# Fewer, larger groups of TensorE transposes in a gated cross-attention and mixture kernel

## The reference, cut to what matters

```
x = x + tanh(g_xattn) * cross_attention(layernorm(x), ctx)     # x: 4 x 512 x 1024
z = layernorm(x)
base  = z @ W_base.T + b_base                                  # 1024 x 1024
gate  = softmax(z @ W_gate.T)                                  # 8 experts
thr   = sigmoid(z @ W_thr + b_thr) * 0.125
w     = relu(gate - thr), normalised to sum 1
h     = z @ A_w.T                                              # 8 experts x rank 16 = 128
moe   = 2 * sum over experts of w * (h @ B_w.T)
out   = x + tanh(g_ffn) * (base + moe)
```

## Time and profile before

| | |
|---|---|
| three runs | 472.96, 473.60, 475.18 us; median 473.6 |
| profiled execution, first to last instruction | 473.6 us |
| TensorE busy | 468.0 us (99%) |
| DVE busy | 361.7 us (76%) |
| ACT busy | 173.8 us (37%) |
| POOL busy | 119.8 us (25%) |
| granted TensorE clock, mean | 1.000 |

### The profile page before, as it was taken

How to read it: one execution, slowest core, us unless ns; L and a number is a source line. 1 busy time by engine, 2 the same in 40 slices (tenths; PEclk the granted TensorE clock), 3 DMA queues, 4 the chain that set the end, 5 groups by cost and what they waited for, 6 DMA issues and landing times.

```text
span 473.6 us, 6945 instructions
## 1 busy us (share of the span) xinstructions
PE 468.0 (99%) x2481; PEld 399.3 (84%) x2481; DVE 361.7 (76%) x750; ACT 173.8 (37%) x349; POOL 119.8 (25%) x107
## 2 busy tenths in 40 slices
PE   8999999999999999999999999999999999999997
PEld 7898999998887888888888888878888888888886
DVE  1687996588888978879987888968777678877733
ACT  5847532332224305226334625342241421414300
POOL 0020511002344253345242406031230502205000
PEclk9999999999999999999999999999999999999999
DMA  8993129958576378576379640221405032050202
GB/s 320 412 408 118 76 90 389 405 183 286 197 246 248 133 252 283 193 292 229 141 273 419 277 144 36 81 98 46 133 1 175 4 89 90 2 177 1 89 1 89
DMA packets 22114, 84.40 MB, mean 178 GB/s; under 512 B 2624, under 2 KB 3904, under 8 KB 19264
## 3 DMA queue, kind: packets, MB, share of 16 engines
q1 hardware_dynamic: 21792, 83.81, 48.2%
q10 hardware_dynamic: 288, 0.15, 0.1%
HBM read 61.93 MB, written 22.02 MB: 177 GB/s over the span
## 4 chain that ended last, share of the span: by engine, by line
PE 78%; DVE 8%; DMA 8%; issue 3%; ACT 1%; POOL 1%; SPq 0%; DVEq 0%; ACTq 0%
PE bank L769 10%; PE bank L773 10%; PE bank L771 10%; PE bank L649 6%; PE bank L685 5%; PE bank L687 5%; PE bank L686 5%; PE bank L530 4%; PE bank L742 4%; DMA xst<-x_dram 3%; DMA T_low<-t_low_T 2%; DMA xz<-xt_dram 2%; DMA out_dram<-xs 2%; PE bank L599 2%; DVE wl_B L1438 1%
## 5 line engine op out<-in xcount | busy, mean ns | idle before, releaser
L1554 POOL TENSOR_TENSOR small<-small,tiny 128x1 f32<-128x1 f32 (+2 forms) x25 | 23.6, 942 | 167.1 <-DVE small L1183 137.9
L1534 DVE SCALAR_TENSOR_TENSOR xs<-bank,tiny,xs 128x512 f32<-128x512 f32 (+1 forms) x61 | 43.3, 739 | 20.6 <-PE bank L773 14.9
L685 PE MATMUL bank<-xth,gram 128*128 128x512 f32 x144 | 57.3, 398 | 0.0
L687 PE MATMUL bank<-xtl,gram 128*128 128x512 f32 x144 | 56.3, 391 | 0.0
L686 PE MATMUL bank<-xth,gram 128*128 128x512 f32 x144 | 56.1, 390 | 0.0
L769 PE MATMUL bank<-wh_B,zh 128*128 128x512 f32 x116 | 47.0, 405 | 0.1
L769 PE MATMUL bank<-wh_T,zh 128*128 128x512 f32 (+1 forms) x116 | 46.6, 402 | 0.0
L1582 POOL TENSOR_TENSOR sq_sum<-sq_sum,sq 128x512 f32<-128x512 f32 x24 | 32.0, 1333 | 56.5 <-DVE sq L1362 56.5
L773 PE MATMUL bank<-wh_B,zl 128*128 128x512 f32 x116 | 45.6, 393 | 0.0
L771 PE MATMUL bank<-wl_B,zh 128*128 128x512 f32 x116 | 45.4, 391 | 0.0
L773 PE MATMUL bank<-wh_T,zl 128*128 128x512 f32 (+1 forms) x116 | 44.7, 386 | 0.0
(11 more groups left out here) (200 smaller groups left out, 1133.2 us busy)
## 6 DMA issues: line engine op xcount, KB each, us to landing
xst<-x_dram SPq DMA_DIRECT2D x16, 512.0 KB, 4.4
xz<-xt_dram SPq DMA_DIRECT2D x16, 512.0 KB, 7.6
out_dram<-xs SPq DMA_DIRECT2D x14, 512.0 KB, 2.7
xa<-x_dram SPq DMA_DIRECT2D x12, 512.0 KB, 3.4
x<-xa SPq DMA_DIRECT2D x12, 512.0 KB, 3.0
xs<-x SPq DMA_DIRECT2D x12, 512.0 KB, 4.0
wq_raw<-wq_dram SPq DMA_DIRECT2D x8, 512.0 KB, 13.8
t_raw_T<-wb_dram SPq DMA_DIRECT2D x4, 1024.0 KB, 16.7
```

The lines of the kernel that those rows point to most:

```text
L685: pe.matmul(acc[:, :], gram[:, g, 0, :], xth[b % 2][:, r, :], start=r == ROWS[j][0], stop=False)
L687: done = pe.matmul(acc[:, :], gram[:, g, 0, :], xtl[b % 2][:, r, :], start=False, stop=r == ROWS[j][-1])
L1534: dve.scalar_tensor_tensor(out=xs[slot][:, cols], in0=bank[n_bank][:, 0:hi - lo], scalar=tg[:, 1:2], in1=xs[slot][:, cols], op0=ALU.mult, ...
```

## The change

It alters the list `stages` and the order in which the low parts of a pair are numbered.

1. `mt` of the two tiles: in pairs 2, 3, 4 and 7 they stood behind P2 and behind P6, one transpose each; both now stand behind P6. Pairs 1, 5 and 6 had both in one place already.
2. `zt` of a11 and a12, for the next pair, in pairs 1 to 6: they stood behind P7 and behind P3, four transposes each; both now stand behind P3, eight in a row.
3. With them move, on ACT and DVE, the high and low parts and all sums. DVE's order behind P7 and P3 was: low a11, s3, s2, low s1, low s3, low a12, s4, low s2, low s4. It is now: low a11, s3, s2, low a12, s4, low s1, low s3, low s2, low s4. Pair 0, which prepares pair 1, keeps the old order.

```diff
-        LOWS = ("a22", "a11", "s1", "s3", "a12", "s2", "s4")
+        LOWS = [("a22", "a11", "s1", "s3", "a12", "s2", "s4")] * (PLAIN + 1)
+        LOWS += [("a22", "a11", "a12", "s1", "s3", "s2", "s4")] * (NP - PLAIN - 1)
...
-            for name in (() if plain(p) else LOWS):
+            for name in (() if plain(p) else LOWS[p]):
...
                              3: [("zt", q, "a21"), ("zt", q, "a22"), ("xn", t1), ("sum_high", q, "s1"), ("bias", t0)],
-                             4: [("zt", q, "a11"), ("sum_high", q, "s3"), ("sum_high", q, "s2"), ("sum_low", q, "s1"),
-                                 ("sum_low", q, "s3")],
-                             5: [("zt", q, "a12"), ("sum_low", q, "s2"), ("sum_high", q, "s4"), ("bias", t1)],
+                             5: [("zt", q, "a11"), ("zt", q, "a12"), ("sum_high", q, "s3"), ("sum_high", q, "s2"),
+                                 ("sum_low", q, "s1"), ("sum_high", q, "s4"), ("bias", t1), ("sum_low", q, "s3"),
+                                 ("sum_low", q, "s2")],
                              6: [("sum_low", q, "s4")]}
...
-                extra = {2: [("mt", t), ("mt", t + 1)]} if attends else {1: [("mt", t)], 2: [("mt", t + 1)]}
+                extra = {2: [("mt", t), ("mt", t + 1)]}
```

## The result

| | before | changed |
|---|---|---|
| median of 6 runs | 473.97 us | 477.84 us |
| lowest to highest | 472.96 to 475.18 | 475.20 to 479.78 |

The ratio is 1.008, with a 95% interval of 1.006 to 1.0101: 3.9 us slower, where 4.4 was forecast (478.0 us). The changed kernel's six runs spread over 4.6 us, the six of before over 2.2; in the larger sets measured beside the experiments the kernel before spreads over 4.6 to 5.4 us.

The account below looks back on a forecast made before the run. TensorE was taken as the bound, with the store and load loop nearly as tight. Late loads cost 4.5 us in pairs 2 to 6, less 0.1 saved: +4.4 on 473.6 gives 478.0 us, range 474.5 to 481.0.

Parts of the forecast that it names:

- What bounds the kernel: TensorE, busy 99% with one wait of 0.2 us; nearly as tight, the loop from `fin` through stores and load to transposes.
- The saving on TensorE: Ten groups of transposes fewer on TensorE were to save 0.1 us, with bounds of -0.2 to 0.3.
- `fin` 2.2 us late, and not in pair 1: On DVE nine steps behind the eight transposes delay `fin` by 2.2 us; in pair 1 it is 0.2 us earlier.
- The delay passes to the landing, and from there to the transposes: The 2.2 us passes through stores and load to the second tile's landing in pairs 3 to 6, then stalls TensorE.
- The terms: TensorE's stalls in pairs 2 to 6: 0.2, 0.7, 0.8, 2.1 and 0.7 us, adding up to 4.5 us.
- The merging of `mt` makes it worse: The first four transposes now wait for the second tile too, not only the second four, which had 0.43 us more.
- The base: The time the loss is added to: the profiled span of 473.6 us, equal to the median of the runs.
- The delay isn't lost on the way: Rival: the delay gets lost between `fin` and landing, only pair 5 pays 0.1 to 2.4 us, 473.7 to 476.0; chance 0.18.
- the groups aren't dear: Rival: each group removed on TensorE gives back 0.3 us or more, 3.0 for ten, time 470.8 us; chance 0.04.
- the transfers didn't get slower by 1 us: Rival: stores and loads overlap worse by 1 us a pair, adding 4 us, time 482 us; chance 0.12.
- the formula: Loss for landing delay d: 0.2 + (d - 1.51) + (d - 1.38) + (d - 0.13) + (d - 1.46), no bracket below nothing.
- only pair 5 pays: With the landing delay under 1.7 us, pairs 3, 4 and 6 keep their room of 1.4 to 1.5 us each.

Follow-up runs that it names:

- store_late: The kernel before, with a pair's first store on SP waiting for all four `fin` additions instead of two, so stores and loads are 1.4 us late: 477.04 us, ratio 1.0081.
- fins_first: The changed kernel with DVE's low parts of s3, s2 and s4 put behind the four `fin` additions: 472.89 us, ratio 0.9977.
- fins_split: The kernel before, split groups kept, with DVE's low parts of s2 and s4 put behind the four `fin` additions: 473.50 us, ratio 0.9988.
- mt_only: The kernel before with only the `mt` transposes merged behind P6; the `zt` groups stay as they were: 473.85 us, ratio 0.9999.
- stores_together: The changed kernel with only SP's order changed, storing both tiles of a pair before loading two: 473.38 us, ratio 0.9982.
- stat_late: The changed kernel with the second tile's `stat` moved on DVE behind `part` of P6 and the low parts of `mt`: 474.80 us, ratio 1.0035.
- zt_only: The changed kernel with the `mt` transposes back behind P2 and P6, so only the `zt` groups are merged: 476.23 us, ratio 1.0054.
- fins_first_2: The same kernel as fins_first, run again: 473.23 us, ratio 0.9974.
- both_split: The kernel before, split groups kept, with low parts of s2 and s4 behind `fin` and the second tile's `stat` behind the low part of `mt`: 475.26 us, ratio 1.0057.

## Why the prediction was right, point by point

- *What bounds the kernel.* Right. With no wait at all six pairs take 171.32 us in the old order; before had 171.81, so 0.5 us of waits in its whole stretch. The loop through store and load was the second bound, and shown to be: 1.4 us on it in every pair, and nothing else, cost 3.8 us (store_late).
- *The saving on TensorE.* The term was mis-sized: 0.1 us predicted, 0.48 measured. It lies outside the stated bounds of -0.2 to 0.3. The pairs with two groups fewer became 0.08 to 0.10 us shorter, those with one fewer 0.03, 0.07 and 0.11, and 0.45 of the 0.48 us lies behind the pair's first group of eight, where only the `zt` groups differ. The step that failed is the product with no transposes, taken as 2.78 us from one place. From the first group of eight to the second, with two products between, it is 6.33 to 6.42 us in fins_first; the group and its product are 3.61 to 3.67 in fins_split; that leaves 2.70 to 2.75 for the product without. The whole pair, read with and without, would have been the better row, but only a control has it. The 1.7 us estimated from the Trainium skill's constant for an isolated matmul (page "TensorE: Matmul & The Clock Gate", section "Single matmul latency", where it is given for bf16) isn't there either: nine of the ten groups lie in these pairs, and 0.48 us for nine is 0.05 each, not 0.17.
- *`fin` 2.2 us late, and not in pair 1.* Right: 6.73 us from the eight transposes to `fin` in pair 3, where 350.29 to 357.04 was reckoned. The first store moved by 2.15 us against the next pair's start (from 0.40 ahead of it to 1.75 behind), and behind pair 1 it came 0.2 us earlier (1.75 behind the start of pair 2 instead of 1.96). That pair 1 isn't late holds in all profiles; the sign of the 0.2 isn't shown, since mt_only, with the old order there, has 1.31.
- *The delay passes to the landing, and from there to the transposes.* Right, and shown from both ends: take the delay away on DVE (fins_first) or on SP (stores_together), and the loss is gone; take away the link between landing and transposes (stat_late), and pairs 2 to 4 lose theirs.
- *The terms.* Reckoned 0.2, 0.7, 0.8, 2.1, 0.7 for pairs 2 to 6; the profile has 0.15, 1.01, 1.15, 1.84, 0.62, with the saving in them. Pairs 3 and 4 are 0.3 us worse since their tiles landed 2.5 and 2.6 us late, not 2.2: in this execution the second store in pair 3 took 5.26 us instead of 5.02, and the load in pair 4 took 3.80 instead of 3.20. The sum, 4.73, is from one execution; the runs say 3.9. In pair 5 the reckoning took the second `mt` transpose to start at 398.65; by the earlier trace rows it is 398.73 (398.62, and 0.38 less the 0.27 of one record). The pair lost 1.91 us without the saving, for a landing 2.03 us late, so the room of 0.13 was about right all the same.
- *The merging of `mt` makes it worse.* Right in direction and in size: with the late landings taken off, it adds 0.43 and 0.42 us in pairs 3 and 4 (changed less zt_only), the 0.43 us by which the first four transposes stand ahead of the second four. Alone it costs nothing.
- *The base.* The profiled span was taken as the device time. For the changed kernel the same execution has 478.0 us and a span of 476.2: 1.8 us lie outside, as in every run whose span is on record (1.75 to 1.88). So the profiled execution of before took about 475.4, some 1.4 us more than the median. That the total came out within 0.2 us is partly luck: the base was 0.4 us too low (473.6 for 473.97) and the sum 0.5 too high (4.4 reckoned, 3.9 measured).
- *The rivals.* The delay isn't lost on the way, the groups aren't dear, and the transfers didn't get slower by 1 us as a rule: the second stores in pairs 2 to 6 took 5.0, 5.3, 5.0, 6.1 and 5.1 us, before 5.0, 5.0, 5.2, 6.3 and 5.1. Two of the figures beside the rivals don't follow from the formula: 0.3 us either way on the delay gives 476.8 to 479.2, not 476.3 to 479.7, and at a delay of 1.7 us pairs 3, 4 and 6 already pay 0.8 us together, so "only pair 5 pays" holds up to 1.4.

The experiments point to a version that beats both: the merged groups with three low parts behind `fin` (fins_first), 0.9977 of before, 0.9961 to 0.9992, and when run again 0.9974, 0.9946 to 1.0002, which just doesn't exclude no gain.

## What to carry to other kernels

Before work is bunched on the engine that is the bound, look at what the next engine does behind it: bunching leaves that engine idle first and puts its whole work in one run, and whatever stands last in its queue (here the additions that release a store and a load) is late by most of that idle time (2.2 us here), though every operand of the bound engine is still in time. Put what starts a long round trip ahead of what only has to be ready by the next stage. And a wait of 0.2 us on the bound engine can hide a loop with no room left: follow the chain that ended last through the transfers and note the room at each place before anything on it is moved.

## What was not expected of the hardware

- Merging groups saves 0.03 to 0.11 us of TensorE's time in a pair (0.48 us over six merged groups of `zt` and three of `mt` in pairs 1 to 6), 0.05 us for each group that is gone, beside the 0.108 us that each transpose takes in a stream.
- The second 512 KB store, beside a load of the same size, landed between 4.4 and 6.7 us after its issue, for the same instruction in pair 5 (4.4 in fins_first_2, 4.6 in fins_first, 4.8 in store_late, 6.3 before, 6.7 in both_split). The first store, alone, took 2.6 to 2.7 us nearly everywhere.
- Five executions with the merged groups and no wait agree in pairs 1 to 6 to 0.01 us (170.83 to 170.84), while over all profiled executions the start of pair 1 lies between 269.8 and 274.9 us. Much of the kernel's spread is made ahead of the part that the change touches.
- Part of that spread is TensorE's clock. The two latest starts of pair 1 are zt_only (274.9) and fins_first_2 (274.6). In both TensorE waited 2.6 and 2.5 us for DVE near 150 us, and the matmuls behind it then stood 0.43 us apart instead of 0.23 for some 3.5 us: the granted clock fell to the lower of its two levels (1.2 instead of 2.4 GHz). In zt_only, 152 to 154 us, with the clock in the third column from the end:

```profile
PE bank L531 <- DVE px L1395: 2.6, 1, 2.6
152.00:154.00 2.00, 2.00 (x6) 1.52 (x6) 1.93 (x6) 0.00 (x0) 1.38 (x2) 0.50 0.58 162
```

  In fins_first, which has no such wait, the clock stays at 1.00 there. The seven runs on record with a mean clock of 0.996, four of them of the kernel before, took 476.55 us or more, against medians of 473.4 to 474.1 for the kernel before.
